# A first projection stage written anew: latent one block ahead, tables read once, tokens loaded early

## The reference

```python
q = (x @ W_q)                       # 256 x 256, 16 heads of 16
lat = x @ W_dkv                     # 256 x 64
lat = (lat - mu) * rsqrt(var + LN_EPS) * ln_gamma + ln_beta
k = (lat @ W_uk); v = (lat @ W_uv)  # 64 x 256 each
q = apply_rope(q); k = apply_rope(k)
```

## Time and profile before

| | us |
|---|---|
| median of 3 runs | 5320.7 |
| the three runs | 5313.73, 5340.69, 5320.7 |
| profiled execution, span | 5307.5 |
| PE, DVE, ACT, POOL busy in the span | 4955.1, 4498.3, 3777.1, 315.1 |
| first projection stage | 2 to 198 |
| its PE busy time | 143.12 |

### The profile page before, as it was taken

The page is one execution under the profiler, slowest core; times in us unless marked ns, Lnnn a source line. Parts: engine busy times, 40 slices in busy tenths (PEclk is TensorE's granted clock), DMA queues, the critical chain, the costliest instruction groups (busy, mean ns, idle before and its releaser), DMA issues. The chain is left out here.

```text
span 5307.5 us, 101793 instructions
## 1 busy us (share of the span) xinstructions
PE 4955.1 (93%) x42036; PEld 2017.7 (38%) x42036; DVE 4498.3 (85%) x5080; ACT 3777.1 (71%) x7189; POOL 315.1 (6%) x482
## 2 busy tenths in 40 slices
PE   7699999999999588877999999999999999999998
PEld 4333433433333245542333333333333333333343
DVE  3688889889886579849999999999999999999346
ACT  2177778787787422232888888888888888888853
POOL 3200000000000011130000000000000000000030
PEclk7589999999998789996999999999999999999999
DMA  4301010010000000051100001000010000000000
GB/s 131 107 23 28 11 29 21 14 40 11 11 8 7 21 17 13 10 196 39 43 5 8 5 4 43 8 5 5 11 37 8 5 5 8 8 4 5 9 1 32
DMA packets 138202, 131.30 MB, mean 25 GB/s; under 512 B 61803, under 2 KB 96491, under 8 KB 137707
## 3 DMA queue, kind: packets, MB, share of 16 engines
q1 hardware_dynamic: 137738, 124.80, 8.3%
HBM read 76.75 MB, written 46.66 MB: 23 GB/s over the span
## 5 line engine op out<-in xcount | busy, mean ns | idle before, releaser
L915 DVE TENSOR_REDUCE att_mx<-ps 128x2 f32<-128x1024 f32 (+2 forms) x3200 | 3746.5, 1192 | 263.1 <-PE ps L801 185.1
L898 ACT ACTIVATE att_probs<-ps 128x512 f32<-128x512 f32 (+3 forms) x6400 | 3385.5, 583 | 596.3 <-PE ps L839 284.5
L864 PE MATMUL ps<-att_probs,att_V 128*17 128x256 f32 (+1 forms) x25088 | 1958.6, 387 | 0.3
L839 PE MATMUL ps<-att_Q,K 50*128 50x512 f32 (+3 forms) x6400 | 1686.9, 492 | 43.9 <-ACT att_probs L898 21.0
L801 PE MATMUL ps<-K,att_Q 48*128 48x512 f32 (+2 forms) x6400 | 1397.3, 414 | 91.7 <-DVE att_mx L915 54.7
L839 PEld LDWEIGHTS ps<-att_Q,K 50*128 50x128 f32 x6400 | 657.0, 185 | 1395.2 <-ACT att_probs L898 1269.7
L864 PEld LDWEIGHTS ps<-att_probs,att_V 128*17 128x17 f32 x25088 | 425.5, 95 | 1065.1 <-issue 597.3
L801 PEld LDWEIGHTS ps<-K,att_Q 48*128 48x128 f32 x6400 | 651.1, 192 | 173.6 <-DVE att_mx L915 122.1
L726 POOL TENSOR_SCALAR_AFFINE_SELECT att_probs<-att_probs 128x512 f32<-128x512 f32 x128 | 81.2, 635 | 1512.8 <-ACT att_probs L898 1512.8
L1169 PE MATMUL ps<-wguT,mlp_xqT 128*128 128x512 f32 (+1 forms) x384 | 159.7, 566 | 0.6 <-DVE mlp_h L1277 0.2
L1368 POOL MEMSET mix_power<- 128x1 f32 x1 | 0.1, 98 | 2655.1 <-POOLq L131 2655.1
(11 more groups left out here) (207 smaller groups left out, 2383.1 us busy)
## 6 DMA issues: line engine op xcount, KB each, us to landing
att_Q<-qhi_scratch SPq DMA_DIRECT2D x256, 64.0 KB, 2.3
K<-khi_scratch SPq DMA_DIRECT2D x256, 64.0 KB, 2.3
v_scratch<-proj_vpad SPq DMA_DIRECT2D x16, 544.0 KB, 3.4
att_V<-v_scratch SPq DMA_DIRECT2D x64, 136.0 KB, 2.5
att_Q<-qlo_scratch SPq DMA_DIRECT2D x128, 64.0 KB, 2.3
K<-klo_scratch SPq DMA_DIRECT2D x128, 64.0 KB, 2.4
proj_x<-in_L_attn_x SPq DMA_DIRECT2D x8, 512.0 KB, 5.4
qhi_scratch<-proj_qhipart SPq DMA_DIRECT2D x16, 256.0 KB, 3.0
```

What stands on the lines that cost most here:

```text
L839: mm = pe.matmul(ring(at)[:, lo:QB], K[rows, par_of(u), j, kt * P:(kt + 1) * P], Q[rows, slot_of(u), j, lo:QB], start=True, stop=True)
L864: mm = pe.matmul(ps[VW * h:VW * h + HV, 6, lo:(part + 1) * (QB // 2)], V[:, par_of(v), kt, HV * h:HV * (h + 1)], probs[:, (n_key[v] + kt) ...
L898: act.activation(probs[:, (n_key[u] + kt) % PBUFS, column(h), lo:QB], ring(at)[:, lo:QB], ACT.Exp, scale=SCALE).then_inc(emptied, 1)
L915: dve.tensor_reduce(mx[:, min(u % NQB, 1), :, j, qt, c], ps[:, 2 + 2 * pair:4 + 2 * pair, 0:max_width(u, i) // 2], AX.X, ALU.max).then_inc ...
```

## The change

`project` no longer serves layer 0. A new function, `project_first`, does the same arithmetic with other orders and waits:

- PE works one latent ahead. After the q rows of block i it makes the latent of block i + 1, then k and the first half of v of block i, transposes the tokens of block i + 2, makes the second half of v, transposes tables and normed latent of block i + 1, and makes its q rows. The waits on `w_set` move from the start of PE's program to the first q rows.
- The tables are read once, whole, by two transfers ahead of the loop; `widen` reads slices of that tile.
- `load(j)` waits for the transposes of block j - 2 alone. It stands four blocks ahead in the loop, behind `store_v`.
- The rows of ones for the keys are stored from a tile of 1024 instead of 2048 elements.
- POOL: rotate q, rstd of the next block, rotate k, widen. DVE: angle q, leave k, measure of the next block, angle k, norm of the next block, leave q. ACT follows PE's order, with the casts between evictions.
- xT's buffer no longer waits for v; latT waits for k too.

```diff
@@ -528,6 +528,364 @@
+def project_first(nc, core, ps, ident, x_dram, w, tables, q_parts, k_parts, v_dram, ones_to):
...
+        tab = sb("tab", [P, 2, NT, half])
+        ones = sb("ones", [PARTS, 1024])
...
+        turns = [("x", 0, 0), ("x", 1, 0)]
+        for i in range(-1, NB - 1):
+            if i + 2 < NB:
+                turns += [("x", 0, i + 2), ("x", 1, i + 2)]
+            turns += [("t", 0, i + 1), ("t", 1, i + 1), ("lat", 0, i + 1)]
+        number = {what: n for n, what in enumerate(turns)}
+        LAT_STEPS = 2 * TB + 1
...
+                def load(j):
+                    if j >= 2:
+                        sp.wait_ge(s["turned"], number["x", 1, j - 2] + 1)
+                    sp.dma_start(x_in[:, j % 2], x_dram[tok(j, B), :].rearrange("(g p) d -> p g d", p=P)
+                                 ).then_inc(x_got[j % 2], 16)
...
+                load(0)
+                for dst, src in [(w_lat[:], w["w_dkv"].rearrange("(c p) e -> p c e", p=P)),
+                                 (wq[:], w["wq"].rearrange("(c p) e -> p c e", p=P)),
+                                 (w_uk[:], w["w_uk"]), (w_uv[:], w["w_uv"]),
+                                 (gb[:, 0:1], w["gamma"].rearrange("(p a) -> p a", a=1)),
+                                 (gb[:, 1:2], w["beta"].rearrange("(p a) -> p a", a=1))]:
+                    sp.dma_start(dst, src).then_inc(s["w_in"], 16)
+                load(1)
+                for m in range(2):
+                    sp.dma_start(tab[:, m], tables[m].rearrange("(g p) d -> p g d", p=P)).then_inc(s["tab_in"], 16)
+                load(2)
+                sp.wait_ge(s["ones_set"], 1)
+                for b in range(2):
+                    rows = ones_to[b * HALF + SROWS:b * HALF + MROWS].bitcast(F32).rearrange("p g j t -> p (g j t)")
+                    sp.dma_start(rows.rearrange("p (r n) -> p r n", n=1024),
+                                 ones[:].unsqueeze(1).to_broadcast([PARTS, 4 * T // 1024, 1024])).then_inc(s["ones_in"], 16)
+                load(3)
+                for i in range(NB):
+                    if i >= 1:
+                        store("k", 1, i - 1)
+                    store_v(i)
+                    if i + 4 < NB:
+                        load(i + 4)
+                    store("q", 0, i)
+                    store("q", 1, i)
+                    store("k", 0, i)
+                store("k", 1, NB - 1)
...
+                def turn_x(j):
+                    pe.wait_ge(x_got[j % 2], 16 * (j // 2 + 1))
+                    for c in range(DC):
+                        dst = ring(number["x", c, j])
+                        for g in range(TB):
+                            mm = pe.transpose(dst[:, g * P:(g + 1) * P], x_in[:, j % 2, g, c * P:(c + 1) * P], ident[:])
+                        mm.then_inc(s["turned"], 1)
+
...
+                def latent(j):
+                    pe.wait_ge(s["kept"], number["x", 1, j] + 1)
+                    if j >= 1:
+                        pe.wait_ge(s["lat_normed"], j)
...
+                def rows_k(j):
+                    pe.wait_ge(s["kept"], number["lat", 0, j] + 1)
+                    if j >= 1:
+                        pe.wait_ge(prods["k"], j * 2)
+                    for m in range(2):
+                        mm = pe.matmul(of["k"][:, m, :], w_ukp[:, m, :], latT[:], start=True, stop=True)
+                    mm.then_inc(made["k"], 1)
+
+                def tokens_v(j, part_of):
+                    if 2 * j + part_of >= 1:
+                        pe.wait_ge(s["v_kept"], 2 * j + part_of)
+                    for g in range(2 * part_of, 2 * part_of + 2):
+                        mm = pe.matmul(ps[:, 6, (g % 2) * D:(g % 2 + 1) * D], latT[:, g * P:(g + 1) * P], w_uv[:],
+                                       start=True, stop=True)
+                    mm.then_inc(made["v"], 1)
+
+                pe.wait_ge(s["w_in"], 16 * 6)
+                turn_x(0)
+                for i in range(-1, NB):
+                    if i + 1 < NB:
+                        latent(i + 1)
+                    if i >= 0:
+                        rows_k(i)
+                        tokens_v(i, 0)
+                    if i + 2 < NB:
+                        turn_x(i + 2)
+                    if i >= 0:
+                        tokens_v(i, 1)
+                    if i + 1 < NB:
+                        turn_tables(i + 1)
+                        turn_latent(i + 1)
+                        rows_q(i + 1)
...
+                    if kind == "x":
+                        if j >= 2:
+                            act.wait_ge(made["q"], j - 1)
+                        act.activation(xT[:, j % 2, m, :], src, ACT.Copy).then_inc(s["kept"], 1)
+                    elif kind == "t":
+                        if j >= 2:
+                            act.wait_ge(prods["k"], 2 * (j - 1))
+                            act.wait_ge(prods["q"], 2 * (j - 1))
+                        act.activation(tabT[:, j % 2, m, :], src, ACT.Copy).then_inc(s["kept"], 1)
+                    else:
+                        if j >= 1:
+                            act.wait_ge(made["v"], 2 * j)
+                            act.wait_ge(made["k"], j)
+                        act.activation(latT[:], src[0:LAT], ACT.Identity, bias=gb[:, 1:2], scale=gb[:, 0:1]
+                                       ).then_inc(s["kept"], 1)
...
+                act.wait_ge(s["w_in"], 16 * 6)
+                for c in range(DC):
+                    keep(("x", c, 0))
+                for i in range(-1, NB):
+                    if i >= 0:
+                        keep_v(i, 0)
+                    if i + 2 < NB:
+                        for c in range(DC):
+                            keep(("x", c, i + 2))
+                    if i >= 0:
+                        keep_v(i, 1)
+                    if i + 1 < NB:
+                        for m in range(2):
+                            keep(("t", m, i + 1))
+                    if i >= 0:
+                        cast("q", i)
+                    if i + 1 < NB:
+                        keep(("lat", 0, i + 1))
+                    if i >= 0:
+                        cast("k", i)
...
+                def widen(j):
+                    if j >= 1:
+                        pool.wait_ge(s["turned"], number["t", 1, j - 1] + 1)
+                    for m in range(2):
+                        ins = pool.tensor_copy(wide[:, m].rearrange("p g (h d) -> p g h d", h=HEADS),
+                                               tab[:, m, tok(j, TB)].unsqueeze(2).to_broadcast([P, TB, HEADS, half]))
+                    ins.then_inc(s["widened"], 1)
+
+                pool.wait_ge(s["tab_in"], 32)
+                widen(0)
+                for i in range(-1, NB):
+                    if i >= 0:
+                        rotate("q", i)
+                    if i + 1 < NB:
+                        pool.wait_ge(s["lat_steps"], (i + 2) * LAT_STEPS)
+                        if i >= 0:
+                            pool.wait_ge(s["lat_normed"], i + 1)
+                        pool.tensor_tensor(rstd[:], var[:], power[:], ALU.pow).then_inc(s["lat_rstd"], 1)
+                    if i >= 0:
+                        rotate("k", i)
+                    if i + 2 < NB:
+                        widen(i + 2)
...
+                for i in range(-1, NB):
+                    if i >= 0:
+                        angle("q", 0, i)
+                        angle("q", 1, i)
+                    if i >= 1:
+                        leave("k", i - 1)
+                    if i + 1 < NB:
+                        measure(i + 1)
+                    if i >= 0:
+                        angle("k", 0, i)
+                        angle("k", 1, i)
+                    if i + 1 < NB:
+                        norm(i + 1)
+                    if i >= 0:
+                        leave("q", i)
...
-        project(nc, core, ps, ident, 0, x0, None, w0, (t["cos0"], t["sin0"]), q_parts, k_parts, v_dram, K)
+        project_first(nc, core, ps, ident, x0, w0, (t["cos0"], t["sin0"]), q_parts, k_parts, v_dram, K)
```

173 lines of the change are left out of this document (added).

## The result

The changed kernel takes 5245.07 us (median of four runs, 5243.41 to 5257.91). The kernel before takes 5326.57 us in the same comparison (four runs, 5313.73 to 5340.69). The ratio is 0.985, with a 95% interval of 0.982 to 0.9875. Forecast: 5260, between 5243 and 5300.

What follows compares the result with a forecast made beforehand. In the first stage, TensorE's waits and low clock were taken as the bound. 23.9 + 7 x 13.0 + 18.6 + 4 = 137.5 us against 198.0 saves 60.5: span 5247, plus 13.2 outside it, 5260 us, range 5243 to 5300.

Steps and rivals of the forecast that it cites:

- Where the time is: First projection stage, 2 to 198 us: the change can only be worth a part of these 196 us.
- The block: One block of the first stage: 13.0 us instead of 21.9, with the latent's transpose waiting for VectorE's norm.
- The 0.3 us that I put on DMA and semaphores: Allowance per block for nearly bound DMA and unmodelled semaphore gaps, raising 12.7 us to 13.0.
- Waits that go: TensorE's token wait, about 1 us a block, goes; v and latT evictions hide; the tables' DMA is gone.
- The clock: TensorE in the first stage: high clock mostly, with one fall at some 4 us.
- The rule weighed against this: Transposes do not engage the full clock, so 2.5 us of them per block would pull it down each time.
- The tables: Two 128 KB table reads at the start: 8 us from issue to landing, between 4.3 and 34, landed by 15.7.
- Start: Stage start until TensorE is free after the first q rows: 23.9 us, against 22.2 before.
- End: From the last block's q rows to the next stage: 18.6 us, where the same end took 22.3.
- the clock falling in every or every other block: Rivals: blocks of 19.5 us, 17 saved, 5304, chance 0.14; or mean 16.2 us, 41 saved, 5280, chance 0.16.
- the cycle stays at 22 us: Rival: an overlooked wait leaves the first stage's blocks unchanged, 5320 us in all; chance 0.04.
- Stores as the bound: Rival: stage data moves only at 135 GB/s, blocks of 24.5 us, 16 us slower, 5337; chance 0.04.

Runs made afterwards that it cites:

- E7: Changed kernel with the latent's norm chain moved ahead on VectorE and rstd ahead of rotate q on GpSimd: stage 123.6 us, median 5257.76 us, ratio 0.986.
- E3: Changed kernel with the token loads put back late, block i + 2 at the head of iteration i: stage 147.1 us, time 5274.64 us.
- E11: Changed kernel unaltered, timed again: median 5249.12 us, ratio 0.985 to the kernel before, stage 125.0 us.
- E9: Kernel before, unedited, profiled once more: stage 200.4 us, time 5307.85 us.
- E1: Kernel before with the first layer's tables read whole by two DMAs ahead of the loop: stage 191.3 us, time 5331.71 us.
- E12: Changed kernel with the tables read per block again in 16 KB pieces, three blocks ahead: stage 125.6 us, time 5254.66 us.

## Why the prediction was right, step by step

**Where the time is**: right. 71 us go from the first stage. Against 5320.7 that is a ratio of 0.987, inside both intervals.

**The block**: right mechanism, 13.0 forecast, 12.1 measured. The latent took 1.8 us at clock 1.00, near the lower of its two bounds (1.7 and 3.4). LatT starts 8.2 us after the q rows, not 8.6 to 8.9, and its wait for the norm is 0.44 us, not about 1. Close behind the norm stands a wait for which the prediction had no term, latT for ScalarE's eviction of the tables: it is why taking the norm forward in E7 brought 0.1 us and not 0.44. The 0.3 us that I put on DMA and semaphores was not there, at a DMA share of 0.79 in the block from 68.5 to 80.6 us:

```profile
68.50:80.60 12.10, 11.66 (x59) 7.53 (x57) 9.25 (x19) 5.88 (x10) 8.98 (x8) 1.00 0.79 263
```

**Waits that go**: right. After has no token wait; E3 brings it back at 2.3 us and the stage to 147. The v eviction hides under the token transposes, except in the last two blocks, which have no tokens to transpose; there it is 0.69 us in the open.

**The clock**: right, but for the size of the fall. It is at 1.00 from 25 to 100 us. A fall came at 102.6 us, in the first block without token transposes, behind its 0.69 us wait, and lasted to 106 us. E11, the same kernel once more, has the same wait and no fall there:

```profile
100.95 1.13 PE L706 MATMUL ps<-proj_wuv,proj_latT 64*128 64x256 f32 x4 [0.69 <-ACT proj_vpad L764]
102.00 1.09 PE L662 MATMUL ps<-ident,proj_wide 128*128 128x128 f32 x8
```

From this latent to the end of the q rows took 12.98 us in after and 12.20 in E11, so the fall cost 0.8 us, not 4. The 4 had no row behind it. A second fall, at 112.8, slows only the last v half, 2.05 us for 1.13, and the stage's end does not wait for that: it hangs on the rotations and casts.

The rule weighed against this, that the full clock does not engage for transposes (the Trainium skill, TensorE: Matmul & The Clock Gate, "Part 4: PE-mode transpose"), would by the prediction's reading have had it fall in each block. The trace disagrees with that reading: each block has 20 transposes, 2.5 us of them, and the clock stayed at 1.00 for six of them in a row. The 5.2 us of transposes and gaps in the earlier trace rows ran at 1.00 too; what a long stretch of transposes alone would do, no run here shows.

**The tables**: 8 us guessed between 4.3 and 34; 7.6 measured, landed at 14.8 instead of 15.7. The nearer row was the better guide. Not foreseen: the issues of the second table and of the load behind it held SP for 3.58 and 3.00 us.

**Start**: 23.9 forecast, 23.7 measured, where the next latent starts. **End**: 18.6 us after the last q rows forecast, 17.9 measured (109.2 to 127.1). The 175.7 that the prediction took for the end of the last q rows before is some 0.4 us early (that group starts at 171.28 and takes 5.05); it enters no term of the sum.

**The sum**: 137.5 forecast, 127.1 measured, so 70.9 us saved instead of 60.5. Of the 10.4 us, 5.5 are the seven blocks (85.5 us with the fall in them, against 91), 4 the extra term for the fall, 0.9 start and end.

**From span to median**: wrong. I took the 13.2 us between the profiled span (5307.5) and the median of the runs as time outside the span. Execution by execution only 1.7 to 2.4 us lie outside (5256.2 and 5257.91 for after, 5306.1 and 5307.85 for E9, 5329.3 and 5331.71 for E1). The profiled execution of before was a short one. With the right stage this would have given 5307.5 - 70.9 + 13.2 = 5250, which is near the medians (5245 and 5249) because the median scatter happens to carry over, not because the reason was right.

**The rivals**: the clock falling in every or every other block is refuted by the 75 us at 1.00. That the cycle stays at 22 us is refuted by the blocks of 12.1. Stores as the bound are refuted too: 263 GB/s ran in the block above, against the 135 on which that rival rested.

What stays open: why some executions have 230 us of low clock in the first attention and others 300, with the same instructions. The runs give no event at which the two part.

## What to carry to other kernels

Where one engine both waits and runs at a low clock, price the two edits together: here early loads of tokens and tables brought 10 to 12 us, fillers that lift the clock 3 to 6, and both 42 to 45, because a faster engine only reaches sooner the event that the other edit would have moved. Start a long detour over other engines (here statistics, rstd and norm) as the first thing after a dense stretch and put independent matmuls over it, and keep the next input's load out from behind a store that waits for a late engine. Take what lies outside the span from one execution's own span and time, never from a median against another execution's span.

## What the runs showed of the hardware

- The matmuls of 64 moving columns, one weight load each, follow the granted clock as the wide ones do: 16 in 3.4 us at 0.50 and in 1.8 at 1.00.
- A wait of 2.28 us (E3) was followed by the low clock, while 0.44 us a block (after) was not. A wait of 0.69 us was followed by it at 102.6 us in after and not in E11; that fall cost 0.8 us.
- A table read of 128 KB in 32-byte pieces kept SP issuing for 3.58 us and the token load behind it for 3.00, against 0.58 and 0.37 at the same places with reads of 16 KB (E12). Two later reads of 16 KB took 2.13 and 2.10.
- GpSimd's 128x4 power took 1.93 us in E7, beside VectorE's subtraction of two SBUF operands, and 1.01 us away from it; the 128x512 rotation took 2.17 against 1.26 in the same way.
- The same attention code, in the windows above, took 1630 to 1667 us from execution to execution. A profiled pair alone would have put 24 us of this scatter down to the change.
